# Two unread products ahead of every slot of the last four steps on TensorE

## The chip, the cores and the metric

The kernel runs on one core of a Trainium2 chip. The metric is the device time of one execution in microseconds; lower is better. A core has TensorE (PE in the rows), VectorE (DVE), ScalarE (ACT), GpSimd (POOL) and SyncE (SP), each with an instruction stream of its own. They are ordered among each other only by semaphores. PEclk is the clock that TensorE was granted, as a share of 2.4 GHz: 0.5 is 1.2 GHz.

## What is computed

Two transformer blocks over 16 batches of 128 tokens of width 128, with a context of 77 rows per batch. All is fp32. The reference, cut:

```python
x = x + tanh(g_xattn[0]) * L0_xattn(ctx, layernorm(x), mask, ...)   # first attention: 16 heads of 64, keys = ctx and x
x = x + tanh(g_ffn[0])   * L0_ffn(layernorm(x), ...)                # up 128 -> 512, butterflies, gelu, down
x = x + tanh(g_xattn[1]) * L1_xattn(layernorm(x), ctx, ...)         # second attention: 16 heads of 8, top 32 of 77 keys
x = x + tanh(g_ffn[1])   * L1_ffn(layernorm(x), ...)                # route each token to one of 8 experts
```

In the second attention each head keeps the 32 largest of its 77 scores. In the last block each token goes through the expert with the largest router probability, `gelu(x @ W1[e]) @ W2[e]`, times that probability.

## The kernel before

The program has a set-up, a staged loop over the batches, and a part over 23 tiles of tokens sorted by expert.

**The loop** is a software pipeline of steps i = 0 to 20 (NB is 16). In step i the batch i is prepared (P), batch i-1 is in the first attention (A), i-2 ends it and goes through the feed-forward (A2), i-3 starts the second attention (B), i-4 ends its top-k (C), and i-5 is finished and routed (E). Steps 0 to 6 on TensorE, and 16 to 20 on every engine, are written out; the others are a loop. A step has 8 slots, 0 to 7. Each engine has a function `step` that says what it issues in each slot, in this order; nothing else sets the order. An engine may be slots ahead of another as far as the semaphores let it.

Step 16 is the last with a first attention (batch 15). In steps 17 to 20 there remain:

- step 17: the last quarter of batch 15's attention and its feed-forward (A2), batches 14 (B), 13 (C), 12 (E)
- step 18: batches 15 (B), 14 (C), 13 (E)
- step 19: batches 15 (C), 14 (E)
- step 20: batch 15 (E)

**TensorE's parts in these steps**: `down` (the feed-forward's second product, L908) and `second_probs_T` (transposes of a quarter of the second attention's weights, L716, read `p`) in slot 0; `attend` (L874), `contexts` (weights by values, L945), `second_T` (transpose of b_z) and `project_out` (L884) in slot 1; `queries` (L921), `second_scores` (L928) and `context_T` (transpose of c_z) in slot 2; `second_out` (L960) in slot 3; `router_T` (transpose of r_z) in slot 5; `hidden` (L899) and `logits` (the router's product, L972) in slot 7; more `contexts` and `second_probs_T` in slots 3, 4 and 6. `count_rows` (L1011 to L1019) counts tokens per expert: in slot (17, 5), in (20, 4) and behind the loop.

**VectorE** does the top-k of the second attention: for each head four rounds of MAX8 (L1558, `m`) and MATCH_REPLACE8 (L1564, `sw`), half of a batch's in its B step from slot 3 on and the rest in slots 0 to 2 of its C step; and the norms and residuals between (L1523 residuals, L1588 and L1590 c_z, L1536 b_z, f_z and r_z). **ScalarE** does exponentials and copies out of the accumulation banks, all through the helper line L1189. **GpSimd** does subtractions, reciprocal roots and, from step 18 on, the scatters of finished rows (L617), one DMA for each batch; the one of batch 15 stands behind the loop.

**Banks.** There are 8 accumulation banks of 128 x 512 fp32. S0 and S1, the two `score_banks`, hold the scores of the first attention, which VectorE (maxima) and ScalarE (exponentials, semaphore exp_done, 8 for each batch) read. After batch 15's last exponential they are free, but for `count_rows`: S0 takes the places of tokens, and S1 the totals, behind the loop only. `reach(pe, name, b, n)` waits until a semaphore has the value that stands for the n-th event of batch b. `w_exp` holds the feed-forward's first weight, loaded at the start and not written again, `ident` is the unit matrix.

Behind the loop come `count_rows(2)`, the map from tiles to experts on VectorE, the last scatter, and the expert tiles.

Of the kernel before, what the change touches and what calls it, by code (L numbers as in the profile page):

```python
# [21 lines left out]
SLOTS = 8  # L22
LAGS = 6

def flamingo_kernel(nc, t, out):
    NB, S, D = t["x"].shape
# [18 lines left out]
    ROW = 2 * D + 2  # L45
    COEF, TOKEN = 2 * D, 2 * D + 1
    NOWHERE = 1 << 20
    ROUTES = ((0, 11), (11, 15), (15, NB))
    assert S == 128 and D == 128 and DH == 64 and HID == 512 and NK * 4 <= 512

    with ExitStack() as ctx:
        def sb(name, shape, dt=F32):
            return ctx.enter_context(nc.sbuf_tensor(name, shape, dt))
# [6 lines left out]
        ident = sb("ident", [128, 128])  # L60
# [14 lines left out]
        w_exp = sb("w_exp", [128, HID])  # L75
# [130 lines left out]
        def banks(name, n):  # L206
# [3 lines left out]
        S0, S1 = SC[:, 0, :], SC[:, 1, :]  # L210
# [5 lines left out]
                   exp_done=8, inv_ready=4, p_norm=4, pt_psum=4, pt_ready=4, z_psum=4, z_ready=4, o_psum=1,  # L216
# [19 lines left out]
        def reach(eng, name, b, n):  # L236

            if b is None:
                return
            value = b * PER[name] + n  # L240
            if not isinstance(b, int) or value > 0:
                eng.wait_ge(s[name], value)
# [40 lines left out]

        PLACE_AT = {(18 + b // 8, b % 8): (b,) for b in range(ROUTES[0][1])}
        PLACE_AT[20, 6] = tuple(range(*ROUTES[1]))

# [107 lines left out]
        def _(pool):  # L394
# [5 lines left out]
            g.memset(no_row[:, 0:TOKEN], 0.0).then_inc(s["c_norow"], 1)  # L400
            g.memset(no_row[:, TOKEN:ROW].bitcast(I32), NOWHERE).then_inc(s["c_norow"], 1)
            g.iota(token_no[:, :], pattern=[[128, NB]], base=0, channel_multiplier=1).then_inc(s["c_token"], 1)
# [205 lines left out]
            def place_row(b):  # L608

                n = [k for k, (b0, b1) in enumerate(ROUTES) if b0 <= b < b1][0]  # L610
                pool.wait_ge(s["place_ready"], n + 1)
# [100 lines left out]
        def _(pe):  # L712
            mm = nc.tensor.matmul
# [15 lines left out]
            for e in range(4):  # L729
                n = 2 * PST * HC  # L730
# [10 lines left out]
            n = 8 * HC  # L741
# [259 lines left out]
            def count_rows(n):  # L1001

                b0, b1 = ROUTES[n]
                if n == 0:
                    pe.wait_ge(s["c_past"], 2)
                    reach(pe, "exp_done", NB - 1, SLOTS)
                else:
                    pe.wait_ge(s["place_ready"], n)
                rows = chosen[:, :, :].rearrange("p b e -> p (b e)")
                pe.wait_ge(s["chosen_ready"], n + 1)  # L1010
                last = mm(S0[:, b0 * NE:b1 * NE], before_p[:, :], rows[:, b0 * NE:b1 * NE], start=True, stop=b1 == 1,  # L1011
                          skip_group_check=True)
                for k in range(1, b1):
                    b = max(b0, k)
                    last = mm(S0[:, b * NE:b1 * NE], ones_bf[:, :], rows[:, (b - k) * NE:(b1 - k) * NE], start=False,
                              stop=(k == b1 - 1), skip_group_check=True)
                if b1 == NB:
                    for b in range(NB):
                        last = mm(S1[:, 0:NE], ones_bf[:, :], chosen[:, b, :], start=(b == 0), stop=(b == NB - 1))  # L1019
                last.then_inc(s["count_psum"], 1)  # L1020

            def step(i, at):
                now["at"] = at
                P, A, A2, B, C, E = (at(n) for n in range(6))
                for slot in range(SLOTS):
                    if i == 17 and slot == 5:
                        count_rows(0)
                    if i == 20 and slot == 4:
# [110 lines left out]
                now["step"] += 1  # L1139

            run_steps(pe, step, LAGS + 1)

            count_rows(2)
# [43 lines left out]
        def _(act):  # L1187
# [98 lines left out]
            def route_exps(n):  # L1286
                b0, b1 = ROUTES[n]
                act.wait_ge(s["r_biased"], n + 1)
                fn(route[:, b0:b1, :], route[:, b0:b1, :], ACT.Exp, scale=-1.0).then_inc(s["r_exp"], 1)
# [132 lines left out]
        def _(dve):  # L1422
# [178 lines left out]
            def route_biases(n):  # L1601

                b0, b1 = ROUTES[n]
                if n == 0:
# [198 lines left out]
```

## Time and profile before

| | us |
|---|---|
| median of three runs | 732.41 |
| lowest, highest | 731.75, 734.16 |
| the profiled execution | 734.37 |
| its span | 732.6 |
| mean granted clock | 0.92 |

| engine | busy us | share |
|---|---|---|
| TensorE, products | 651.1 | 89% |
| VectorE | 571.1 | 78% |
| ScalarE | 481.2 | 66% |
| GpSimd | 446.9 | 61% |

A share over the whole span mixes stages with different limits. Where a stage is to be judged, its own windows and waits are read, and in this kernel also the granted clock of the stage.

### The profile page before, as it was taken

How to read it: one execution, taken by the hardware profiler on the slowest of the kernel's cores; microseconds unless marked ns; L12 is line 12 of the kernel's file. 1: busy time of each engine (PE TensorE's matmuls, PEld its weight loads, DVE VectorE, ACT ScalarE, POOL GpSimd, SP SyncE). 2: the span in 40 equal slices, each digit the busy share in tenths (PEclk: the TensorE clock that was granted, in tenths of full speed). 3: DMA queues.
4: the chain of work that ended last, by engine and by line, in shares of the span. 5: the costliest groups of instructions: out<-in, count | busy, mean ns of one | idle time of the engine just before them, and what ended most of it. 6: DMA issues, size and time to landing. Idle time of an engine off the chain costs nothing.

```text
span 732.6 us, 19295 instructions
## 1 busy us (share of the span) xinstructions
PE 651.1 (89%) x4994; PEld 529.2 (72%) x4994; DVE 571.1 (78%) x3740; ACT 481.2 (66%) x1331; POOL 446.9 (61%) x689
## 2 busy tenths in 40 slices
PE   5588999999999999999999999999999876772995
PEld 4455677778787787878787878778786764551995
DVE  3255747898989999998989898999999998943231
ACT  1247578888878797888878887878787634221221
POOL 7364667857657575756576765757575536543344
PEclk9779999999999999999999999999999755555998
DMA  7300039992000000000000000000000000003772
GB/s 204 76 1 1 1 105 309 318 294 70 1 3 1 1 1 0 0 0 0 0 0 0 0 0 0 0 0 0 0 1 2 1 0 28 32 23 116 210 205 64
DMA packets 38537, 37.92 MB, mean 52 GB/s; under 512 B 3633, under 2 KB 34249, under 8 KB 38484
## 3 DMA queue, kind: packets, MB, share of 16 engines
q1 hardware_dynamic: 32986, 27.76, 13.6%
q10 hardware_dynamic: 3994, 6.36, 3.1%
q0 software_dynamic: 1504, 3.17, 1.2%
q8 instruction: 24, 0.39, 0.2%
q14 instruction: 29, 0.24, 0.1%
HBM read 16.28 MB, written 21.45 MB: 52 GB/s over the span
## 4 chain that ended last, share of the span: by engine, by line
PE 49%; DVE 35%; issue 6%; POOL 3%; SPq 3%; DMA 2%; ACT 2%; DVEq 0%; POOLq 0%
DVE sw L1564 14%; DVE m L1558 9%; PE bank L716 8%; PE bank L874 6%; PE bank L816 5%; PE bank L945 5%; PE bank L884 4%; PE score_banks L846 3%; DVE negmax L1511 3%; PE bank L1161 3%; PE bank L1171 3%; PE bank L826 2%; PE bank L804 2%; PE bank L908 2%; PE bank L899 2%
## 5 line engine op out<-in xcount | busy, mean ns | idle before, releaser
L1564 DVE MATCH_REPLACE8 sw<-m,sw 128x77 f32<-128x77 f32 x1024 | 219.6, 221 | 0.1
L1558 DVE MAX8 m<-sw 128x8 f32<-128x77 f32 x1024 | 188.8, 225 | 2.3 <-ACT sw L1189 1.3
L1189 ACT ACTIVATE prob<-score_banks,negmax 128x205 f32<-128x205 f32 x256 | 107.2, 431 | 21.3 <-DVE negmax L1511 21.3
L485 POOL TENSOR_TENSOR prob<-prob,inv 128x820 f32<-128x820 f32 x64 | 99.4, 1553 | 18.7 <-DVE inv L1516 18.7
L504 POOL TENSOR_TENSOR sw<-sw,m 128x616 f32<-128x616 f32 x64 | 77.9, 1217 | 50.1 <-DVEq L1545 49.7
L945 PEld LDWEIGHTS bank<-v,p1T 77*128 77x128 f32 x512 | 72.6, 216 | 16.3 <-DVE c_z L1590 6.1
L945 PE MATMUL bank<-v,p1T 77*128 (+1 forms) x512 | 72.5, 269 | 10.9 <-DVE c_z L1590 5.4
L1564 DVE MATCH_VALUE_LOAD sw<-m,sw 128x8 f32 x1024 | 76.6, 75 | 0.0
L1511 DVE TENSOR_REDUCE negmax<-score_banks 128x2 f32<-128x410 f32 x128 | 68.1, 573 | 2.7 <-PE score_banks L846 2.7
L716 PE MATMUL bank<-ident,prob 128*77 128x128 f32 (+1 forms) x512 | 67.3, 275 | 1.6 <-POOL prob L485 1.4
L1189 ACT ACTIVATE h_ring<-bank 128x256 f32<-128x256 f32 (+1 forms) x87 | 38.5, 443 | 45.5 <-PE bank L1161 35.5
L826 PE MATMUL bank<-raw,kvT 128*77 128x512 f32 (+1 forms) x128 | 66.7, 603 | 0.0
L716 PEld LDWEIGHTS bank<-ident,prob 128*77 128x77 f32 (+1 forms) x512 | 58.7, 146 | 9.3 <-POOL prob L485 5.1
L816 PE MATMUL bank<-kvT,raw 128*128 128x205 f32 x256 | 60.4, 359 | 1.2 <-DVE xs L1523 0.6
L928 PE MATMUL bank<-second_keys,b_q 128*128 128x308 f32 x128 | 53.2, 500 | 9.1 <-ACT p1T L1189 8.8
L846 PE MATMUL score_banks<-k_sb,q_sb 64*128 64x205 f32 x512 | 58.7, 348 | 0.0
L511 POOL TENSOR_TENSOR p<-sw 128x308 f32<-128x308 f32 x64 | 46.9, 733 | 18.4 <-ACT sw L1189 18.2
L874 PE MATMUL bank<-ptc,z_ring 77*64 77x128 f32 x512 | 53.7, 287 | 3.3 <-issue 2.6
L816 PEld LDWEIGHTS bank<-kvT,raw 128*128 128x128 f32 x256 | 43.2, 192 | 16.1 <-issue 14.5
L1189 ACT ACT_TABLE_LOAD x34 | 43.6, 1283 | 15.9 <-issue 15.3
L1189 ACT ACTIVATION_READ_ACCUMULATOR prob<-score_banks,negmax 128x1 f32 x256 | 52.9, 207 | 0.0
L874 PE MATMUL bank<-ptl,z_ring 128*64 128x128 f32 x512 | 50.6, 274 | 0.0
(235 smaller groups left out, 1446.7 us busy)
## 6 DMA issues: line engine op xcount, KB each, us to landing
z_sorted<-no_row SPq DMA_DIRECT2D x1, 17415.0 KB, 65.6
raw<-in_L_ffn_W ACTq DMA_DIRECT2D x23, 256.0 KB, 3.4
z_ring<-z_sorted SPq DMA_DIRECT2D x23, 129.0 KB, 3.4
w<-in_L_ffn_W SPq DMA_DIRECT2D x8, 256.0 KB, 4.5
raw<-in_L_xattn_Wkv SPq DMA_DIRECT2D x2, 512.0 KB, 11.2
xs<-in_x SPq DMA_DIRECT2D x1, 960.0 KB, 7.2
cx<-in_ctx SPq DMA_DIRECT2D x1, 577.5 KB
raw<-in_L_xattn_Wq SPq DMA_DIRECT2D x1, 512.0 KB, 10.4
```

What stands on the lines that cost most here:

```text
L485: g.tensor_tensor(p, p, inv[:, 4 * q:4 * q + 4].unsqueeze(2).to_broadcast([128, 4, KV]), ALU.mult).then_inc(s["p_norm"], 1)
L504: g.tensor_tensor(v, v, m8[:, 4 * q:4 * q + 4, 0, 0:1].to_broadcast([128, 4, 2 * NK]), ALU.subtract).then_inc(s["sub_done"], 1)
L716: return nc.tensor.transpose(dst, src, ident[0:rows, 0:rows])
L816: last = mm(dst[:, KV * c:KV * c + KV], wkv_in[:, at:at + 128], kvT[:, :], start=True, stop=True)
L826: mm(dst[0:nr, :], kvT[:, r0:r0 + nr], wkv_in[:, INNER + 512 * j:INNER + 512 * j + 512], start=True, stop=True)\
L846: last = mm(SC[:, u, KV * r:KV * r + KV], q_sb[rows[u], q // 2, 2 * (q % 2) + r, :], k_sb[rows[u], q % 2, r, :], start=False, stop=(r == 1 ...
L874: last = mm(dst[64 * u:64 * u + 64, 128 * c:128 * c + 128], v[:, DH * h:DH * h + DH], p[:, 2 * c + u, :], start=not last_part, stop=last_p ...
L945: last = mm(M[:, c:c + D1 + 1], p1T[:, n, :], v1[:, bass.ds(b, 1), 4 * q + n, :].squeeze(1), start=True, stop=True)
L1189: return nc.scalar.activation(dst, src, f, **kw)
L1511: v.tensor_reduce(negmax[:, 2 * p:2 * p + 2], SC[:, :, KV * (p % 2):KV * (p % 2) + KV], AX_X, ALU.max, negate=True).then_inc(s["max_ready" ...
L1558: v.max(m8[:, h, r, :], sw[:, h, src, :]).then_inc(s[name], 1)
L1564: v.match_replace(sw[:, h, 1, :], m8[:, h, r, :], sw[:, h, src, :], TAKEN)\
```

## The change

In steps 17 to 20 (i > NB), at the start of each of the 8 slots, TensorE does two products: `ident` as the stationary operand, `w_exp` (128 x 512, fp32) as the moving one, into the whole of S1. Nobody reads what they write. The first of the 32 pairs waits until batch 15's exponentials are done. These are 64 products in all.

```diff
+    FILL = 2
...
+            def keep_busy():
+
+                for n in range(FILL):
+                    mm(S1[:, :], ident[:, :], w_exp[:, :], start=True, stop=True, skip_group_check=True)
+
             def step(i, at):
                 now["at"] = at
                 P, A, A2, B, C, E = (at(n) for n in range(6))
                 for slot in range(SLOTS):
+                    if i is not None and i > NB:
+                        if (i, slot) == (NB + 1, 0):
+                            reach(pe, "exp_done", NB - 1, SLOTS)
+                        keep_busy()
                     if i == 17 and slot == 5:
                         count_rows(0)
```

TensorE at the end of step 16 and in slots (17, 0) and (17, 1), before. `prob` is batch 15's last quarter, `p` the second attention's weights, `wd,f_h` the down projection.

```order
L716 MATMUL bank<-ident,prob 128x128
L716 MATMUL bank<-ident,p 77x128 [waits p1_ready,h_ready]
L716 MATMUL bank<-ident,p 77x128 x3
L908 MATMUL bank<-wd,f_h 128x128 [waits h_ready,z_ready]
L908 MATMUL bank<-wd,f_h 128x128 x3
L945 MATMUL bank<-v,p1T 128x9 [waits p1T_ready,lg_ready]
L945 MATMUL bank<-v,p1T 128x9 x3
L716 MATMUL bank<-ident,p 77x128 [waits p1_ready,p1T_ready]
L716 MATMUL bank<-ident,p 77x128 x3
L874 MATMUL bank<-ptc,z_ring 64x128 [waits w_ready,z_ready,pt_ready]
```

The same place now (lines of the new kernel are one to ten higher):

```order
L717 MATMUL bank<-ident,prob 128x128
L1026 MATMUL score_banks<-w_exp,ident 128x512 [waits exp_done]
L1026 MATMUL score_banks<-w_exp,ident 128x512
L717 MATMUL bank<-ident,p 77x128 [waits p1_ready,h_ready]
L717 MATMUL bank<-ident,p 77x128 x3
L909 MATMUL bank<-wd,f_h 128x128 [waits h_ready,z_ready]
L909 MATMUL bank<-wd,f_h 128x128 x3
L946 MATMUL bank<-v,p1T 128x9 [waits p1T_ready,lg_ready]
L946 MATMUL bank<-v,p1T 128x9 x3
L717 MATMUL bank<-ident,p 77x128 [waits p1_ready,p1T_ready]
L717 MATMUL bank<-ident,p 77x128 x3
L1026 MATMUL score_banks<-w_exp,ident 128x512 x2
```

A pair stands ahead of the transposes and of the down projection, with the added wait, and another between the next transposes and the attention product.

TensorE in step 20 from slot 0 on, before. `c_z` is the second attention's result, `r_z` the normed row for the router, `wr,r_zT` the router's product.

```order
L716 MATMUL bank<-ident,p 77x128 [waits p1_ready,p1T_ready]
L716 MATMUL bank<-ident,p 77x128 x3
L945 MATMUL bank<-v,p1T 128x9 [waits p1T_ready,lg_ready]
L945 MATMUL bank<-v,p1T 128x9 x3
L716 MATMUL bank<-ident,c_z 128x128 [waits cz_ready]
L960 MATMUL bank<-l_wT,c_zT 128x128 [waits cT_ready]
L1011 MATMUL score_banks<-chosen,before_p 128x32 [waits chosen_ready,place_ready]
```

The same place now:

```order
L1026 MATMUL score_banks<-w_exp,ident 128x512 x2
L717 MATMUL bank<-ident,p 77x128 [waits p1_ready,p1T_ready]
L717 MATMUL bank<-ident,p 77x128 x3
L946 MATMUL bank<-v,p1T 128x9 [waits p1T_ready,lg_ready]
L946 MATMUL bank<-v,p1T 128x9 x3
L1026 MATMUL score_banks<-w_exp,ident 128x512 x4
L717 MATMUL bank<-ident,c_z 128x128 [waits cz_ready]
L1026 MATMUL score_banks<-w_exp,ident 128x512 x2
L961 MATMUL bank<-l_wT,c_zT 128x128 [waits cT_ready]
L1026 MATMUL score_banks<-w_exp,ident 128x512 x2
L1012 MATMUL score_banks<-chosen,before_p 128x32 [waits chosen_ready,place_ready]
```

One pair stands ahead of the transposes, two ahead of that of c_z, and one ahead of each of the next two parts. Behind these rows come, now, a pair, the transpose of r_z, two pairs and the router's product; before, the transpose and the product alone.

## Rows read from the trace of the kernel before

**Rows 1.** The page's 40 slices: busy tenths, and the granted clock

```profile
PE   5588999999999999999999999999999876772995
...
DVE  3255747898989999998989898999999998943231
...
PEclk9779999999999999999999999999999755555998
```

**Rows 2.** Windows: busy us of each engine, TensorE's clock, DMA

```profile
core 0: us, PE busy (x) PEld busy (x) DVE busy (x) ACT busy (x) POOL busy (x), PEclk, DMA share, GB/s
...
575.00:640.00 65.00, 47.15 (x203) 37.64 (x202) 59.55 (x429) 23.44 (x48) 32.68 (x43) 0.58 0.05 17
640.00:663.00 23.00, 14.83 (x71) 12.41 (x71) 11.07 (x72) 4.56 (x12) 10.60 (x16) 0.50 0.05 18
...
588.00:591.60 3.60, 1.35 (x5) 0.74 (x5) 3.41 (x21) 1.70 (x4) 1.80 (x3) 0.97 0.00 0
...
609.00:612.00 3.00, 0.90 (x8) 0.67 (x7) 2.60 (x21) 0.96 (x2) 0.59 (x1) 1.00 0.01 3
```

**Rows 3.** Timeline of TensorE at full clock: start, us, idle before in brackets

```profile
525.72 1.02 PE L826 MATMUL bank<-raw,kvT 128*128 128x512 f32 x2
526.58 0.60 PE L716 MATMUL bank<-ident,p 128*77 128x128 f32 x4
```

**Rows 4.** Timeline of TensorE in steps 17 and 18

```profile
573.57 0.60 PE L716 MATMUL bank<-ident,p 128*77 128x128 f32 x4
574.00 1.06 PE L908 MATMUL bank<-wd,f_h 128*128 128x128 f32 x8
...
578.54 0.69 PE L874 MATMUL bank<-ptc,z_ring 77*64 77x128 f32 x4 [2.08 <-issue]
...
582.85 3.64 PE L884 MATMUL bank<-raw,h_ring 128*128 128x128 f32 x16
...
615.46 0.45 PE L716 MATMUL bank<-ident,b_z 128*128 128x128 f32 x1 [0.45 <-DVE b_z L1536]
616.37 0.77 PE L921 MATMUL bank<-b_zT,l_wT 128*128 128x128 f32 x2 [0.46 <-ACT b_zT L1189]
...
618.67 1.39 PE L928 MATMUL bank<-second_keys,b_q 128*128 128x308 f32 x2 [0.68 <-ACT p1T L1189]
```

**Rows 5.** Timeline of ScalarE and of VectorE around the start of step 17

```profile
568.77 0.43 ACT L1189 ACTIVATE prob<-score_banks,negmax 128x205 f32<-128x205 f32 x1
...
575.91 0.35 DVE L1523 SCALAR_TENSOR_TENSOR xs<-bank,tg,xs 128x128 f32<-128x128 f32 x1 [0.26 <-DVE sw L1564]
```

**Rows 6.** Waits of VectorE from 576 to 646: total, times, longest

```profile
DVE xs L1523 <- PE bank L884: 1.3, 1, 1.3
DVE m L1558 <- ACT sw L1189: 1.3, 1, 1.3
```

**Rows 7.** Timeline of TensorE in steps 19 and 20

```profile
640.31 1.88 PE L945 MATMUL bank<-v,p1T 77*128 77x9 f32 x8 [2.21 <-DVE c_z L1590]
...
646.49 1.88 PE L945 MATMUL bank<-v,p1T 77*128 77x9 f32 x8 [0.73 <-DVE rows_out L1523]
...
654.22 1.85 PE L945 MATMUL bank<-v,p1T 77*128 77x9 f32 x8 [0.77 <-ACT p1T L1189]
656.83 0.45 PE L716 MATMUL bank<-ident,c_z 128*128 128x128 f32 x1 [0.77 <-DVE c_z L1590]
657.73 0.77 PE L960 MATMUL bank<-l_wT,c_zT 128*128 128x128 f32 x2 [0.46 <-ACT c_zT L1189]
...
661.28 0.45 PE L716 MATMUL bank<-ident,r_z 128*128 128x128 f32 x1 [2.32 <-DVE r_z L1536]
662.19 0.56 PE L972 MATMUL bank<-wr,r_zT 128*128 128x8 f32 x2 [0.46 <-ACT r_zT L1189]
```

**Rows 8.** The chain that ended last: the scatter of batch 15's rows

```profile
667.25 2.80 DMA z_sorted<-rows_out,place
```

## The prediction

> **What bounds the kernel now.** I read first the page's 40 slices [rows 1]. VectorE is at 8 to 9 tenths from the start of the attention loop to slice 35. TensorE is at 9 until slice 31, and from slice 32 to slice 36 it is at 6 to 8 while its granted clock is 0.5 to 0.7. So for the last 80 us of the staged loop TensorE runs mostly at 1.2 GHz. This is exactly the part where the change acts, steps 17 to 20. Next I read busy time by window [rows 2]. From 575 to 640 us (steps 17 and 18) VectorE is busy 59.55 of 65 us: two batches' top-k run there, so VectorE sets the pace. From 640 to 663 us (steps 19 and 20) VectorE is busy 11.07 of 23 and TensorE 14.83 of 23, at clock 0.50. There only batches 14 and 15 are left, and what is left of them is a zigzag of TensorE, ScalarE, VectorE. Last I read who waits. VectorE loses 1.3 us to the output projection of batch 15 and 1.3 us to the first second-attention scores of batch 15 [rows 6]; otherwise it waits almost for nothing in steps 17 and 18.
>
> Two things follow. A full clock can give back at most those 2.6 us in steps 17 and 18, plus half of TensorE's time on the path in steps 19 and 20. And the products that are added sit in TensorE's own order, ahead of each slot's work: in steps 17 and 18 they can hide behind VectorE, in steps 19 and 20 there is little to hide behind.
>
> **The price of one added pair.** A 128x512 fp32 product is two instructions in the trace. At full clock the pair at 525.72 us is followed by the next work at 526.58 [rows 3], so one product costs 0.86 us of TensorE and a slot's two cost 1.72. At half clock the same columns take 3.44. Four steps of 8 slots make 64 products: 55 us at full clock. The weight load of ident runs beside the product before it, as it does for that row; I take it at nothing. Nobody reads the bank, and each product starts its own group, so there is no wait among them.
>
> **The one added wait** is exp_done for batch 15 ahead of the first pair. TensorE reaches that place at 573.57. ScalarE's last exponential of batch 15 begins at 568.77 and is 0.43 long [rows 5], four microseconds earlier. Nothing; were it late, the down projection of batch 14 would be queued behind it.
>
> **Steps 17 and 18, 575 to 640 us.** TensorE's own work there is 47.15 us at a mean clock of 0.58 [rows 2]; at full clock that is 27. With 16 pairs of 1.72, 27.5, it is 55 of 65 us. That fits, but no longer loosely, so VectorE should see some arrivals later and some earlier. In order:
> - The pair of (17, 0) stands ahead of the transposes at 573.57 and thus of the down projection of batch 14, which VectorE takes at 575.91, 0.3 us after it is free [rows 5]. The projection began at 574.00 and is 1.06 long [rows 4]; 1.72 later its end is at 576.8. VectorE loses 0.9.
> - The pair of (17, 1) falls mostly into the 2.08 us that TensorE idles before 578.54 [rows 4]. If the clock stays up, the 3.64 us projection at 582.85 takes 1.8 and the 1.3 us that VectorE waited for it are gone. Net so far -0.4.
> - After that TensorE is nearly gapless until step 18. The second output product of batch 12 follows a pair and comes about 0.2 later than VectorE wants it.
> - In (18, 2) the chain b_z, transpose, query product, transposes, scores has one pair inside it, between the transpose and the query product. From 615.46 to the end of the scores, 618.67 and 1.39, it takes 4.6 us, of which TensorE waits 0.46 and 0.68 [rows 4]. The pair adds 1.72 less the 0.46; the full clock takes off 1.7, half of the remaining 3.46; and earlier work in the slot comes sooner. VectorE's 1.3 us wait behind it shrinks, by 0.8 at most, and a later product that follows a pair takes 0.5 of that back.
> The sum to 640 us is -0.3. The bounds are -2.6 (both waits gone, nothing new) and, if the clock falls again in the gaps around 582 and 614, more: the trace has the clock at 0.50 after TensorE's idle 2.08 us, and then up only for the stretches 588 to 591.6 and 609 to 612 [rows 2, 4]. Each stretch at half clock holds TensorE back by half its length, and a pair in it costs 3.44. With 10 us of slack in 65, my estimate is 1.2 us on VectorE's path for one such stretch, and between 0 and 5 for none to several.
>
> **Steps 19 and 20, the deciding part.** The anchor is the context product of batch 15 at 640.31, released by VectorE's c_z [rows 7]. From there to the end of the last router product, 662.19 and its 0.56, the kernel before takes 22.4 us. After it come (19, 2) to (20, 7): 14 pairs, 24.1 us at full clock. TensorE's own work there is 14.83 at clock 0.50 [rows 2]; halved it is 7.4, with the anchor's product in it. Of the waits of before, in brackets in [rows 7] (0.73, 0.77, 0.77, 0.46, 2.32, 0.46, and some more of 0.6 to 0.8), nearly all now pass under a pair: between the transpose of c_z and the product with it, between r_z's transpose and the router, before every context product but one. What has no pair in it is the transposes of (20, 0), ScalarE's copy and the context product, 0.7, and VectorE's residual of batch 14 ahead of the context product at 646.49, 0.5. So the stretch is 24.1 + 7.4 + 1.2 = 32.7 us against 22.4, or +10.3. TensorE would be busy almost without a gap, as it was through the slices 5 to 31, at 8 to 9 tenths or more, in which the granted clock was 9 or more [rows 1]. Therefore I price it at full clock.
>
> Behind the last router product the end is as before: exponentials, choice, counting, placing rows, and the scatter of batch 15 that lands 2.80 us after 667.25 [rows 8], then the expert tiles. No pair stands there and the queues hold the same work, so the shift passes through one for one. TensorE idles on those transfers, as before, so I expect the first expert tiles at half clock as before.
>
> **What the skill says.** In this trace the work behind the 2.08 us of idling, outside two short stretches, is at 1.2 GHz [rows 2, 4]. The Trainium skill, page TensorE: Matmul & The Clock Gate, in its closing table under Why this matters for your kernels, advises no idle gaps between bursts of matmuls, since the engine else falls to half rate; by that rule alone the sum would be the gain of the rival below. The same page, in the section Step-by-step: what each phase is for, says that matmuls themselves keep their program order and only weight loads are pulled ahead. By that, a pair whose result nobody wants still holds back what stands behind it, and the sum is the one above. No row here can show a product overtaken.
>
> **The sum.** +10.3 (steps 19, 20), -0.3 (steps 17, 18), +1.2 (one more stretch at half clock) = +11.2 us. The profiled execution took 734.37 for a span of 732.6, so its like after the change is 745.6, span 743.8. The median of the runs before is 732.41, which gives 743.6.
>
> **Rivals.**
> - Faster: the added products vanish in waits and the full clock pays. TensorE's own work in steps 19 and 20 falls from 14.83 to 7.4, and the two waits of VectorE go: up to 10 us off, 722; with half of it hidden anyway 728. This decides by the price of a pair: the stretch of 22.4 us holds 7.4 + 1.2 of other work, so 14 pairs break even at 0.99 us each. The trace shows 1.72. Against it also: the 14 pairs alone exceed the stretch. Chance 0.04.
> - The shift is small, 738.9 to 741: VectorE gets both waits back, the clock never falls, part of the pairs overlaps more than I think. 10.3 - 2.6 = +7.7, 740.1. For it: with 55 of 65 us filled the gaps in which the clock fell are mostly closed. Chance 0.15.
> - The clock swings on in steps 17 and 18: pairs at 3.44 delay the scores and the residuals of VectorE's stage by 3 to 6 us beyond my 1.2. Then +13.5 to +17, 746 to 749.5. For it: by the walk above, idle gaps of 1 to 2 us remain around 582 and 614, and a gap of 2.08 us stood ahead of the fall of the clock in the trace. Chance 0.22.
> - The clock stays down altogether: 14 pairs are 48 us and the own work 14.8, some +41, 773. Against it: TensorE would then be busy without a gap, and the clock did go up again at 588 and at 609 in this trace [rows 2]. Chance 0.03.
> - The change doesn't do what it says: the wide products leave the clock at half only where it doesn't matter, and all is as before within 0.3%. It would need the pairs to be free. Chance 0.02.
>
> **Numbers.** The forecast, 741 to 746, has 0.54; 0.15, 0.22, 0.03, 0.04 and 0.02 go to the rest. About 0.3% is what a measurement of this kernel can tell from no change. Faster by more 0.04, within 0.02, slower by more 0.94. The range from 739.0 to 749.5 takes in the forecast, the small shift and most of the swinging clock.
>
> **What would show it.** Right: the granted clock in slices 32 to 36 near 1; TensorE near 10 of 10 from about 636 to 673 us; VectorE idle there; the last router product near 673 instead of 662.2; a pair 1.7 us long; the stretch from the scatter of batch 15 to the end as long as before. The time of step 17's and 18's VectorE work, about 575.9 to 640, within 2 us of before. Wrong: a pair that costs under 1 us, a clock that stays at 0.5 in steps 19 and 20, or VectorE waits of over 2 us in steps 17 and 18.

## The result and the profile after

| | us |
|---|---|
| median after, 4 executions | 741.53 |
| median before, 4 executions | 732.79 |
| difference | +8.7 |
| ratio, 95% interval | 1.0118, 1.0100 to 1.0136 |
| profiled execution after, its span | 740.46, 738.7 |

The kernel is slower by 8.7 us (7.3 to 10.0 by the interval). The prediction was 743.6 with a range of 739.0 to 749.5; against the median of before it meant +11.2, which lies above that interval. Two single executions of this study, 839.84 us of the kernel before and 1572.95 us of the kernel with products in the gaps, are in a slow state and are left out of every ratio and spread below, though the medians count them.

The slices of the page after, to be laid beside [rows 1]:

```profile
PE   6588999999999999999999999999999888993995
...
DVE  4266639899999989898999999898989998813232
...
PEclk9699999999999999999999999999999998997899
```

The clock does what the change is for (slices counted from 1, as in the prediction): where it stood at 7 and then 5 from slice 32 on, it is at 8 or 9 through slice 36. TensorE is at 8 to 9 tenths there. VectorE is at 1 in slice 36, where it was at 4. The windows that stood for steps 17 and 18 and for steps 19 and 20 in the trace of before (columns as in [rows 2]):

```profile
575.00:640.00 65.00, 57.43 (x268) 35.31 (x267) 59.16 (x437) 21.32 (x45) 32.75 (x41) 0.95 0.05 19
640.00:663.00 23.00, 21.78 (x85) 12.08 (x84) 6.40 (x40) 3.51 (x9) 5.91 (x9) 1.00 0.03 12
```

In the first window VectorE is as busy as before (59.16 of 65 against 59.55). In the second TensorE is busy 21.78 of 23 us and VectorE only 6.40: TensorE is now the limit of that stage.

**Where the time is.** Fixed windows mislead here, since the two profiled executions reach step 17 at different times. The last exponential of batch 15, which lies ahead of everything the change touches, begins at 568.77 before and at 564.62 after:

```profile
564.62 0.43 ACT L1199 ACTIVATE prob<-score_banks,negmax 128x205 f32<-128x205 f32 x1
```

So I cut both traces at three events: that exponential, the context product of batch 15 (slot (19, 1)), and the end of the last router product.

| stretch, us | before | after | change |
|---|---|---|---|
| start to the last exponential | 568.77 | 564.62 | -4.15 |
| to the context product (steps 17, 18) | 71.54 | 73.14 | +1.60 |
| to the end of the last router product (steps 19, 20) | 22.44 | 32.50 | +10.06 |
| to the end of the span | 69.85 | 68.44 | -1.4 |

The same windows as the trace has them (length, TensorE busy, granted clock, DMA share, GB/s), before and then after:

```profile
568.77:640.31 71.54, 53.26 (x262) 0.61 0.04 16
640.31:662.75 22.44, 14.82 (x71) 0.50 0.05 19
```

```profile
564.62:637.76 73.14, 65.44 (x335) 0.95 0.04 16
637.76:670.26 32.50, 31.28 (x128) 1.00 0.06 21
```

The first row of the table isn't the change's work: no instruction ahead of that exponential differs. In the profiles of this study, all with the same code up to there, it begins between 564.6 and 568.9.

Of the +1.60, only 1.0 is delay of VectorE. Its c_z, the last thing it makes ahead of that context product, begins 71.20 us behind the exponential before and 72.21 after; the other 0.6 is TensorE, where the product now stands behind the pair of (19, 1) and begins 0.93 us behind the start of c_z in place of 0.34:

```profile
639.97 0.29 DVE L1590 TENSOR_TENSOR c_z<-bank,c_inv 128x128 f32<-128x128 f32 x1
```

```profile
636.83 0.29 DVE L1600 TENSOR_TENSOR c_z<-bank,c_inv 128x128 f32<-128x128 f32 x1
643.46 1.06 PE L946 MATMUL bank<-v,p1T 77*128 77x9 f32 x8 [0.45 <-DVE rows_out L1533]
```

The last row is the next context product, which VectorE's residual (`rows_out`) releases. It begins 77.72 us behind the exponential before and 78.84 after, +1.1. From there to the end of the last router product it is 16.26 and 26.80 us, +10.5, and this is where the loss is. VectorE's top-k sets the first number, so this is a better place to cut than the anchor, and I come back to it.

VectorE's waits of over 0.3 us from 570 to 646 us after, to be laid beside [rows 6] (total, times, longest):

```profile
DVE m L1568 <- ACT sw L1199: 3.3, 1, 3.3
DVE r_z L1546 <- POOL c_rs L494: 1.2, 1, 1.2
DVE xs L1533 <- PE bank L909: 1.2, 1, 1.2
DVE m L1568 <- DVE sw L1574: 0.6, 2, 0.3
DVE rows_out L1533 <- PE bank L961: 0.4, 1, 0.4
```

The wait for the output projection is gone. In its place there is one of 1.2 for the down projection (L909), which now stands behind the first pair, and the one for the first scores of batch 15 (ScalarE's copy, `m <- sw`) grew from 1.3 to 3.3. The 1.2 us for GpSimd's c_rs, and the 0.4 for L961, belong to step 19 already (645.33 and 643.05). The first was there before too, at 648.35, behind the window of [rows 6].

TensorE in step 20 after (start, us, idle before in brackets), beside the last rows of [rows 7]:

```profile
656.09 1.03 PE L946 MATMUL bank<-v,p1T 77*128 77x9 f32 x8 [0.77 <-ACT p1T L1199]
656.97 3.68 PE L1026 MATMUL score_banks<-w_exp,ident 128*128 128x512 f32 x8
660.49 0.27 PE L717 MATMUL bank<-ident,c_z 128*128 128x128 f32 x1
660.60 1.88 PE L1026 MATMUL score_banks<-w_exp,ident 128*128 128x512 f32 x4
662.32 0.38 PE L961 MATMUL bank<-l_wT,c_zT 128*128 128x128 f32 x2
662.54 1.88 PE L1026 MATMUL score_banks<-w_exp,ident 128*128 128x512 f32 x4
...
666.54 3.60 PE L1026 MATMUL score_banks<-w_exp,ident 128*128 128x512 f32 x8
669.98 0.28 PE L973 MATMUL bank<-wr,r_zT 128*128 128x8 f32 x2
```

The own work takes half of what it took: the product of c_z 0.38 in place of 0.77, the router's 0.28 in place of 0.56. Between them lie the pairs. From 660.60 to the next work at 662.32 a pair takes 1.72 us. In these rows the waits of before are gone, but for the 0.77 ahead of the context product, the one place without a pair.

### The profile page after: what moved, and what is told of

Same layout as the page of the kernel before. It is cut to its first block, busy times and chain, and to the rows that moved or that the text cites. A ratio compares the mean times of both kernels' runs of the same rounds, so it can differ in the third digit from the quotient of the medians.

```text
span 738.7 us, 19551 instructions
## 1 busy us (share of the span) xinstructions
PE 676.9 (92%) x5122; PEld 531.5 (72%) x5122; DVE 570.2 (77%) x3740; ACT 481.7 (65%) x1331; POOL 449.0 (61%) x689
## 4 chain that ended last, share of the span: by engine, by line
PE 53%; DVE 32%; issue 6%; POOL 3%; SPq 2%; DMA 2%; ACT 1%; DVEq 0%; POOLq 0%
DVE sw L1574 12%; DVE m L1568 8%; PE bank L717 8%; PE bank L875 6%; PE bank L817 5%; PE score_banks L1026 5%; PE bank L946 5%; PE bank L885 3%; PE score_banks L847 3%; DVE negmax L1521 3%; PE bank L1171 3%; PE bank L1181 3%; PE bank L827 2%; PE bank L805 2%; PE bank L909 2%
## 5 line engine op out<-in xcount | busy, mean ns | idle before, releaser
L486 POOL TENSOR_TENSOR prob<-prob,inv 128x820 f32<-128x820 f32 x64 | 99.5, 1554 | 18.6 <-DVE inv L1526 18.6
L946 PEld LDWEIGHTS bank<-v,p1T 77*128 77x128 f32 x512 | 63.3, 192 | 9.4 <-issue 4.5
L946 PE MATMUL bank<-v,p1T 77*128 (+1 forms) x512 | 63.3, 251 | 4.4 <-ACT p1T L1199 1.5
L1026 PE MATMUL score_banks<-w_exp,ident 128*128 128x512 f32 x128 | 62.4, 615 | 0.0
L929 PE MATMUL bank<-second_keys,b_q 128*128 128x308 f32 x128 | 48.4, 460 | 8.0 <-ACT p1T L1199 8.0
```

Of the source, the lines that this page charges most:

```text
L486: g.tensor_tensor(p, p, inv[:, 4 * q:4 * q + 4].unsqueeze(2).to_broadcast([128, 4, KV]), ALU.mult).then_inc(s["p_norm"], 1)
L946: last = mm(M[:, c:c + D1 + 1], p1T[:, n, :], v1[:, bass.ds(b, 1), 4 * q + n, :].squeeze(1), start=True, stop=True)
L1026: mm(S1[:, :], ident[:, :], w_exp[:, :], start=True, stop=True, skip_group_check=True)
```

## The experiments

The theory: in steps 17 and 18 the pairs hide behind VectorE for the most part; in steps 19 and 20 each product is paid in full, 0.86 us, and outweighs what the full clock gives. The main rival: the loss comes from steps 17 and 18, from order and from the clock that still falls there. The first five runs are changes to the changed kernel, the others to the kernel before. Stage 1 is from the last exponential of batch 15 to its context product in (19, 1), stage 2 from there to the end of the last router product. The output doesn't depend on the added products in any of them.

### One product in place of two

```diff
-    FILL = 2
+    FILL = 1
```

> One product for each of the 32 slots in place of two. Theory (in steps 19 and 20 each added product costs its 0.86 us on TensorE's order, 12 of the 28 there above the break-even of 0.99 us a slot): the stretch from the context product of batch 15 to the end of the last router product, 22.4 us before and 32.5 after the change, holds 14 x 0.86 = 12.0, 7.4 of own work at full clock, and the waits that a product of 0.86 does not cover, 1.5 to 2.5: 21 to 22 us, so 0.5 to 1.5 us under before, and the time about that of the kernel before, -2 to +1 us, if the clock stays up in steps 17 and 18. Rival (the loss of the change is mostly the added wait, delays in steps 17 and 18 and the clock falling, not the price of the products): the stretch is above 27 us and over half of the 8.7 us loss stays.

Measured: 734.11 against 733.60 us, ratio 1.0017 (0.9993 to 1.0041).

```profile
565.58:638.47 72.89, 55.58 (x298) 0.88 0.05 16
638.47:662.09 23.62, 21.18 (x99) 0.93 0.05 18
```

Halving the products takes away nearly the whole loss, as the theory has it. Its number for stage 2, 21 to 22 us, was too low: it is 23.62. The clock was at half for part of it (0.93), and I had counted the gain of the full clock over the whole of stage 2. The first part of it is bound elsewhere. From the context product to the next one of batch 15 it is 6.18 us before, 5.70 after and 6.33 here: VectorE does the last 5.7 us of top-k there, and the next context product needs the residual behind it. What TensorE does in slots (19, 1) to (19, 3) costs nothing as long as its output product (L961), which the residual reads, is there when the top-k ends, and doing it faster gains nothing. Here the residual waited 0.41 us for it, after 0.36 us in the changed kernel.

### The pairs in steps 17 and 18 alone, and in steps 19 and 20 alone

```diff
-                    if i is not None and i > NB:
+                    if i is not None and NB < i <= NB + 2:
```

> The pairs only in steps 17 and 18. Theory: the stage from batch 15's last exponential to the context product at the head of step 19 is 73.1 us as after the change against 71.5 before (+1.6), and the stretch behind it is as before, 20 to 22.4 us, a little less where the clock is still up at its start. Total +0 to +2 us on before. Rival (the pairs in steps 17 and 18 carry a larger part of the loss): +4 us or more.

```diff
-                    if i is not None and i > NB:
-                        if (i, slot) == (NB + 1, 0):
+                    if i is not None and i > NB + 2:
+                        if (i, slot) == (NB + 3, 0):
```

> The pairs only in steps 19 and 20. Theory: the loss is there: the stage to the context product as before, 71.5 us, the stretch behind it 32 to 34 us (the first pairs may be at half clock, 3.4 us each), total +9 to +12 us on before. Rival as for the pairs in steps 17 and 18 alone: +4 us or less.

Measured for steps 17 and 18 alone: 733.15 against 733.60 us, ratio 0.9995 (0.9976 to 1.0013), no change that the runs can tell, where 0 to 2 us more was expected:

```profile
566.44:638.99 72.55, 62.13 (x327) 0.95 0.04 16
638.99:661.44 22.45, 14.82 (x71) 0.50 0.05 19
```

For steps 19 and 20 alone: 744.11 against 733.60, +10.5, ratio 1.0172 (1.0107 to 1.0238), as expected:

```profile
565.69:637.72 72.03, 56.38 (x270) 0.64 0.04 16
637.72:670.23 32.51, 31.29 (x128) 1.00 0.06 21
```

The rival falls. Without the pairs in steps 19 and 20 stage 2 is 22.45 us, as before to 0.01; with them it is 32.51, as after to 0.01. The clock didn't outlast the pairs either: in the first run it is at 1.00 until 638, falls within the 2.68 us in which TensorE waits for c_z ahead of 638.99, and is at 0.50 over all of stage 2. VectorE's c_z begins 72.20 us behind the exponential there, as in the changed kernel (72.21), and 70.75 in the second run, so the pairs of steps 17 and 18 delay it by 1.0 to 1.5 us. The second run's four executions were 739.4, 740.4, 747.8 and 749.3 us, at mean clocks of 0.948, 0.943, 0.934 and 0.935: the longer ones have the lower clock. Only the first has a trace, so where in the others the clock was down is open; pairs at half clock would cost that much.

### One more product in the gap of step 18

```diff
                         if B is not None:
+                            if i == 18:
+                                mm(S1[:, :], ident[:, :], w_exp[:, :], start=True, stop=True, skip_group_check=True)
                             second_T(B, 3)
```

> As after the change, with one more product of 0.86 us in step 18, between the context product and the transpose of b_z, where TensorE idled 1.22 us at 610. Theory: the granted clock fell to 0.50 from 609 to 615 because of TensorE's gaps of 1.49 and 1.22 us there; with the second gap nearly closed it stays at 1.00, and VectorE's wait of 3.3 us for the scores of batch 15 shrinks to under 1.3. Total 1 to 2.5 us under the changed kernel, though TensorE has more to do. Rival (the wait comes from the pair in the chain and its order, not from the clock): the wait stays 3 us or grows, total equal or up to 1 us more.

Measured: 740.04 against 733.60 us, ratio 1.0096 (1.0065 to 1.0128). Its median is 1.5 us under that of the changed kernel in another session, but the two intervals overlap (1.0100 to 1.0136 there), so the medians alone don't show a gain. Stage 1 is 71.86 us in place of 73.14 in the traces, with TensorE doing more:

```profile
565.72:637.58 71.86, 65.38 (x337) 0.98 0.05 16
637.58:670.08 32.50, 31.28 (x128) 1.00 0.06 21
```

```profile
DVE m L1570 <- ACT sw L1201: 2.0, 1, 2.0
DVE xs L1535 <- PE bank L909: 1.2, 1, 1.2
```

In the changed kernel the rows of the same place are these, with the window of the low clock:

```profile
607.89 1.11 PE L946 MATMUL bank<-v,p1T 77*128 77x9 f32 x8 [1.49 <-DVE c_z L1600]
610.22 0.45 PE L717 MATMUL bank<-ident,b_z 128*128 128x128 f32 x1 [1.22 <-DVE b_z L1546]
```

```profile
608.60:615.40 6.80, 5.55 (x15) 0.51 0.16 58
```

So the clock fell behind the first gap, of 1.49 us, and ahead of the second, of 1.22, which TensorE spent at half clock already. The expectation had both gaps as the cause, and that is wrong: a product put into the second gap could not prevent the fall. It didn't. Here the clock fell too, 0.9 us behind a first gap of 1.50, but it was back after 3.4 us in place of 6.8 (the window 608 to 618 has a mean of 0.83), and VectorE's wait is 2.0 us in place of 3.3. A later run, the one with pairs in steps 17 and 18 and products in the gaps, has the same extra product behind the same first gap of 1.50 us. There the clock did not fall at all, and the wait is 0.80:

```profile
606.00:620.00 14.00, 11.06 (x50) 1.00 0.08 29
```

```profile
617.92 0.38 DVE L1574 MAX8 m<-sw 128x8 f32<-128x77 f32 x2 [0.80 <-ACT sw L1205]
```

Half clock for 6.8, 3.4 and 0 us goes with waits of 3.3, 2.0 and 0.8, with a pair in the chain each time. So the clock makes the greater part of that wait, and not the pair or its order. What decides whether the clock falls behind such a gap is open. That the wait would go under 1.3 in the run of this section was a miss.

### Three products

```diff
-    FILL = 2
+    FILL = 3
```

> Three products for each slot in place of two. Theory: from two on, TensorE is the only limit of the stretch from the context product to the last router product, so each further product of 0.86 us is paid in full: 32.5 + 14 x 0.86 = 44.5 us there. In steps 17 and 18 TensorE's demand becomes 27 + 41 = 68 us of 65, so it sets the pace there too, +4 to +9 us against the changed kernel. Total about +16 to +21 us on the changed kernel. Rival (the stretch is bound by what waits for each other, and products pass partly in gaps): under +8 us there.

Measured: 763.64 against 732.82 us, ratio 1.0417 (1.0384 to 1.0449).

```profile
567.00:648.67 81.67, 77.59 (x370) 1.00 0.05 17
648.67:693.19 44.52, 43.30 (x156) 1.00 0.04 15
```

Stage 2 is 44.52 us, where 44.5 was expected: from two products on each costs its 0.86 in full. Stage 1 is 8.5 us over that of the changed kernel, TensorE busy 77.59 of 81.67 us. The 16 products more are 13.8 us there, so 5.3 of them still went under VectorE's work, and the cover was near its end. The total is 22.1 us over the changed kernel's, where 16 to 21 was expected, a miss by 1.

### Products only in the gaps

If the loss is the length of the products, products no longer than TensorE's waits should give the clock without the cost. Slots and columns by hand, `"0b"` being the place between the transposes and the context product of slot 0. This is a change to the kernel before, cut; the wait for exp_done stands ahead of the products of (19, 1):

```diff
+    FILL = {(19, 1): (512, 512), (19, 2): (512, 512), (19, 3): (512,), (19, 5): (256,), (19, 6): (256,),
+            (20, '0b'): (384,), (20, 2): (384,), (20, 3): (256,), (20, 5): (512, 512), (20, 7): (256,)}
...
+            def keep_busy(at):
+
+                for n in FILL.get(at, ()):
+                    mm(S1[:, 0:n], ident[:, :], w_exp[:, 0:n], start=True, stop=True, skip_group_check=True)
...
+                    if i is not None and i > NB:
+                        if (i, slot) == (19, 1):
+                            reach(pe, "exp_done", NB - 1, SLOTS)
+                        keep_busy((i, slot))
```

> No products in steps 17 and 18. In steps 19 and 20 products only where TensorE waited, and no longer than the wait: pairs of 512 columns in (19, 1), (19, 2), one in (19, 3), 256 columns in (19, 5), (19, 6), (20, 3), (20, 7), 384 between the transposes and the context product of (20, 0) and in (20, 2), two of 512 in (20, 5). Theory (the loss is the length of the products, and the full clock by itself pays): the stage before is as before, 71.5 us; the stretch falls from 22.4 to 17.5 to 19.5 us, own work 7.4 in place of 14.8, and the total is 3 to 5 us under before. Rival (the full clock pays nothing since the path runs through the other engines' latencies): the stretch is 22 us or more, total as before.

Measured: 730.85 against 732.82 us, ratio 0.9968 (0.9951 to 0.9986). The kernel is faster than both, by some 2.3 us against before going by the ratio, where 3 to 5 was expected.

```profile
566.14:638.72 72.58, 55.83 (x267) 0.60 0.04 16
638.72:656.67 17.95, 16.25 (x94) 0.99 0.06 23
```

Stage 2 is 17.95 us in place of 22.44, as the theory says. Stage 1 is 1.0 longer: the pair of (19, 1) ran at half clock, 3.4 us, and ended 1.1 us after c_z was there. But that is no loss, since the next context product waits for VectorE's top-k: it begins 77.79 us behind the exponential, before 77.72. All of the gain lies behind it, 12.74 us in place of 16.26, and up to the last router product the two stages together are 3.4 us shorter. And 2 us go again behind stage 2: VectorE waits 3.25 us, not 1.06, for the last count of rows, which I come to below.

The next run adds pairs in steps 17 and 18 (`{...}` is the table above, `'1b'` the place ahead of the transpose of b_z; the wait for exp_done stands ahead of (17, 1) now):

```diff
-    FILL = {...}
+    FILL = dict([((i, slot), (512, 512)) for i in (17, 18) for slot in range(8) if (i, slot) != (17, 0)] +
+                list({...}.items()) + [((18, '1b'), (512,))])
```

> As the run with products only in the gaps of steps 19 and 20, and pairs in every slot of steps 17 and 18 but (17, 0), with one product more between the context product and the transpose of b_z in step 18. Theory: leaving out (17, 0) takes away VectorE's wait of 1.2 us for the down projection; the stage from batch 15's last exponential to the context product is 70 to 71 us against 71.5 before and 71.9 with all pairs and the extra product. The stretch behind it as in the other run. Total 0 to 1.5 us under that run. Rival (the pairs in steps 17 and 18 cost more through the order than the clock gives): 0.5 us or more above it.

Measured: 733.45 against 732.82 us, ratio 1.0001 (0.9983 to 1.0019).

```profile
566.13:637.67 71.54, 62.15 (x329) 0.98 0.05 16
637.67:658.11 20.44, 18.39 (x93) 0.83 0.06 20
```

Without the pair of (17, 0) VectorE's wait for the down projection is gone, which settles its cause. But the clock fell near 579.7, in a gap of 1.90 us, the output projection took 3.33 us again and VectorE waited 1.0 for it. Stage 1 is 71.54, not 70 to 71. The median is 2.6 us above that of the run without products in steps 17 and 18, so the number is the rival's. Its mechanism isn't what the trace shows. VectorE's c_z begins 71.19 us behind the exponential, 71.23 in the other run, and the context product behind the residual 77.71 and 77.79: the pairs of steps 17 and 18 cost nothing there and gained nothing. The traces part behind that, 14.27 against 12.74 us, where the clock was at half from about 644.5 to 647.5, behind a gap of 1.46 us. Whether that is so in the other executions is not shown.

### A shorter start, a repetition, and narrower products

```diff
-    FILL = {(19, 1): (512, 512), (19, 2): (512, 512), ...
+    FILL = {(19, 1): (512,), (19, 2): (512, 512), ...
```

> As the run with products only in the gaps of steps 19 and 20, but one product of 512 columns in (19, 1) in place of two. There the pair still ran at half clock, 3.4 us, and held the context product back to 1.35 us after VectorE's c_z, against 0.34 before. Theory: one product, 1.7 us at half clock, is over before c_z comes, so the stage before it falls by 1.0 us; the clock rises a little later or as before, and the stretch behind is 17.9 to 20 us. Total 0 to 1 us under that run if the clock still rises by (19, 3), 1 to 2 us over it if not.

> The run with products only in the gaps of steps 19 and 20 once more, on the same chip as the shorter one, to see how steady its gain is: 2 to 3 us under before in the median of the executions, the stretch 17.9 us where the clock rises at (19, 2).

Measured on the same chip: 731.80 for the shorter start and 730.26 for the table as it was, both against 732.94 us; ratios 0.9976 (0.9956 to 0.9996) and 0.9962 (0.9943 to 0.9982). The shorter start, then the other:

```profile
568.88:640.45 71.57, 54.85 (x265) 0.61 0.04 16
640.45:661.14 20.69, 18.98 (x93) 0.86 0.06 20
```

```profile
567.41:639.98 72.57, 55.78 (x266) 0.61 0.04 16
639.98:658.22 18.24, 16.54 (x94) 0.98 0.06 22
```

One product ahead takes the 1.0 us out of stage 1, where it had cost nothing. But the clock rises one pair later, the pair of (19, 2) then takes 3.56 us at half clock, and VectorE's residual waits 2.03 us for the output product behind it. The next context product begins 79.51 us behind the exponential in place of 78.06, and behind it the two traces are alike, 12.75 us each. Stage 2, 20.69 us, is over the expected 20. The total is 1.5 us above the other's, as expected for a late clock, though the two intervals overlap. The gain of the table repeats, -2.7 us.

In the last run only the products of (20, 5) change:

```diff
-            (20, '0b'): (384,), (20, 2): (384,), (20, 3): (256,), (20, 5): (512, 512), (20, 7): (256,)}
+            (20, '0b'): (384,), (20, 2): (384,), (20, 3): (256,), (20, 5): (128,) * 8, (20, 7): (256,)}
```

> As the run with products only in the gaps, but the two products of 512 columns in (20, 5) are eight of 128, the same columns in 12 more instructions. Question: the wait of VectorE for the last count of rows was 3.25 us in that run against 1.06 before, though TensorE did the count in the same time, and this gave back 2 us of the gain. If it comes from where TensorE's instruction stream stands at that moment, it changes with the number of instructions, to about 1.1 us, and the total falls by 2 us. If it comes from the time or from the state of the other engines, it stays at about 3.2 us, and the total is the same within 0.5 us. The stretch to the last router product stays at 17.9 to 18.6 us either way.

Measured: 730.31 against 733.71 us, ratio 0.9953 (0.9930 to 0.9975), the same as the table's two runs within their intervals. VectorE's wait, here, before and after:

```profile
667.11 0.17 DVE L1652 TENSOR_TENSOR place_e<-score_banks,expert_base 128x8 f32<-128x8 f32 x1 [3.24 <-remote]
```

```profile
666.10 0.17 DVE L1639 TENSOR_TENSOR place_e<-score_banks,expert_base 128x8 f32<-128x8 f32 x1 [1.06 <-PE score_banks L1019]
```

```profile
673.49 0.17 DVE L1649 TENSOR_TENSOR place_e<-score_banks,expert_base 128x8 f32<-128x8 f32 x1 [1.00 <-PE score_banks L1020]
```

The wait stays with 12 instructions more, so it isn't the count of TensorE's instructions. In all kernels with two products or more in every slot of steps 19 and 20 it is 1.0 us, as before; with the pairs in steps 17 and 18 alone it is 2.8, with one product a slot 2.1, and with products in gaps 3.1 to 3.3. TensorE's rows of the count are alike in all. What releases it 2 us late is open. In this profile the clock also fell in step 19, with stage 2 at 21.7 us; it was the longest of ten executions (734.2 us). Its stage 2 is a miss against 17.9 to 18.6. The clock fell near 647.7, in a wait of 0.37 us, with no wait over 0.5 us since the pair of (19, 1). TensorE's products up to there are the same as in the two runs of the table, whose clock stayed up.

## Why the prediction was right, point by point

**The price of a pair** (1.72 us at full clock): 1.72 measured, and the run with three products shows the price of one, 0.86, on the path.

**Steps 19 and 20** (+10.3): +10.06. The terms: 14 pairs at 24.1 and own work at 7.4 make 31.5, measured busy 31.28; waits 1.2, measured 0.77 and 0.45. That the clock would be full there is right too (1.00). One thing in it I had not seen: the first 6.2 us were under VectorE's top-k, not under TensorE. It did little harm to the sum, since with two products TensorE was busy nearly without a gap anyway, and it is part of why the expectation for one product missed.

**Steps 17 and 18** (-0.3, and 1.2 for one stretch at half clock, together +0.9): +1.0 at VectorE's c_z, +1.60 at the anchor, where the pair of (19, 1) adds 0.6. The items of the list, the 0.8 taken in full, make -0.5, not -0.3, a slip of 0.2. Down projection 0.9, measured 1.15 as a wait. Output projection: its wait of 1.3 is gone, as forecast. The second output product of batch 12, 0.2: no such wait in step 17. The scores of batch 15: the wait was to shrink to 0.5 and to grow by 1.2 if the clock fell; the clock did fall once, at the place named, around 610, for 6.8 us, and the wait is 3.3. So the mechanism was right and this term too small, by about 1.6. That the sum came out near all the same is in part luck. A wait of VectorE of over 2 us in steps 17 and 18 stood among the signs of being wrong, and this one is over it.

**The added wait** (nothing): right, the first pair stands in the row without idle time.

**One for one to the end** (+0): from the last router product to the end it is 68.44 us in place of 69.85, -1.4. 0.25 of it is plain: before, the last scatter stood in GpSimd's queue behind four others, 0.30 us apart (4.50 us from the router product to the scatter of [rows 8]); after, the four are long gone when it comes (4.25):

```profile
670.78 0.96 POOL L618 DMA_INDIRECT z_sorted<-rows_out,place  x1 [0.30 <-issue]
674.51 0.96 POOL L618 DMA_INDIRECT z_sorted<-rows_out,place  x1 [2.77 <-DVE place L1652]
```

Most of the rest, 1.2, lies behind the first transpose of the expert tiles (674.29 before, 681.58 after): 58.31 us to the end of the span before, 57.12 after. The pairs are not what shortens it. All other traces have 56.6 to 57.5 there, the one whose steps 19 and 20 are as before 56.64, so the single trace of before is the odd one. That the end takes 67.5 to 68.7 us in the four profiles with two products or more in every slot of steps 19 and 20, and 69.2 to 70.7 in the others, comes from this and from VectorE's late count of rows: the scatter is 4.2 to 4.3 us behind the router product in the first group, 4.5 before, and 5.4 to 6.5 in the rest.

**The sum.** From the last exponential to the last router product the profiles show +11.66 where I had +11.2; with the end, +10.3. The medians show +8.7, with the interval up to 10.0, so the forecast sum is 2.5 us too high. Of the 2.9 us between +11.66 and the medians, 0.25 is the scatter, and 1.2 is the tiles, if the trace of before is an odd one there. The remaining 1.5 is open: there is one profile of the kernel before and one of the kernel after, the kernel before varied from 730.3 to 737 us in these sessions, and the part ahead of step 17 alone by 4 us between profiles. The forecast of 741 to 746 held the time, 741.53, near its lower edge; that it did for a sum too high by 2.5 is its width.

**The rivals.** Faster with the full clock: its decisive price of a pair was put at 0.99 us. With one product of 0.86 a slot the time is as before within the interval and stage 2 still 1.2 us longer, so that break-even was too high. It took all of the 22.4 us for TensorE's, and the first 6.2 are not. The swinging clock was right as far as one fall. The rule of program order (the Trainium skill, TensorE: Matmul & The Clock Gate, Step-by-step: what each phase is for) agrees with the rows of step 20 above, where each own product stands only behind its pairs.

## What to carry to other kernels

Work that is added to hold a clock is ordinary work in an engine's order: in these runs it was free only where the engine would have waited anyway, and no longer than the wait. Judge it stage by stage: behind another engine that sets the pace it may cost little and also gain little, and on a chain of latencies it must fit into the gaps one by one. Here 2 x 512 columns ahead of every slot cost 8.7 us, and 256 to 1024 columns in the gaps of the last two steps, where the clock was on the path, won 2 to 3.4, and 1.1 where the clock rose late. And put the cuts between stages where the engine that sets the pace hands over: a delay at another place may be no loss.

## What the runs showed of the hardware that I had not expected

- The granted clock does not carry over: with pairs up to the end of step 18 it was 0.95 in stage 1, fell in the one wait of 2.68 us ahead of the next context product, and was 0.50 over the whole stage 2 that followed.
- The same gap does not always bring the clock down. In step 18 it fell behind a gap of 1.49 or 1.50 us in two of the runs shown and stayed at 1.00 behind one of 1.50 in a third, and in a later run it fell in a wait of 0.37 us, with none over 0.5 us in the 7 us ahead of it.
- Executions of one kernel spread differently: 740.5 to 742.1 us (four executions) with pairs in all four steps, 739 to 749 (four) with the pairs in steps 19 and 20 alone, 727.5 to 734.2 (ten) for the narrow products.
- VectorE's wait for the last count of rows is 1.0 or 2 to 3.3 us by kernel, with the same rows on TensorE, and not by the number of TensorE's instructions. The cause is open.
